# Two mixture-of-experts stages and attention as one program in steps

## The reference

```python
x = x + attn_a(layernorm(x), ...)    # test-time training, two steps with Newton-Schulz; unchanged here
x = x + ffn(layernorm(x), We, be, Wg, bg)
x = x + attn_b(layernorm(x), g, b, w_qkv, w_out, b_out)
x = x + ffn(layernorm(x), We, be, Wg, bg)

def ffn(x, We, be, Wg, bg):          # 8 experts, the best 2 of each token
    gates = softmax(x_flat @ Wg + bg)
    topk_gates, topk_idx = top_k(gates, 2); topk_gates /= sum(topk_gates)
    expert_out = einsum('nd,edo->neo', x_flat, We) + be
    return sum(take_along_axis(expert_out, topk_idx) * topk_gates)

def attn_b(x, g, b, w_qkv, w_out, b_out):   # x (4, 512, 128), 16 heads of 64
    q, k, v = split(((x - mean) / sqrt(var + eps) * g + b) @ w_qkv)
    attn = softmax(where(frame(q) >= frame(k), q k^T / 8, -inf))   # frames of 32 tokens
    return concat_heads(attn @ v) @ w_out + b_out
```

## Time and profile before

| | us |
|---|---|
| median of 3 runs | 888.53 |
| lowest, highest | 884.89, 889.42 |
| the profiled execution, own time | 889.06 |
| its span, first to last instruction | 887.3 |
| mean granted TensorE clock | 0.934 |

### The profile page before, as it was taken

The page is one execution under the profiler, slowest core; times in us unless marked ns, Lnnn a source line. Parts: engine busy times, 40 slices in busy tenths (PEclk is TensorE's granted clock), DMA queues, the critical chain, the costliest instruction groups (busy, mean ns, idle before and its releaser), DMA issues. The chain is left out here.

```text
span 887.3 us, 16341 instructions
## 1 busy us (share of the span) xinstructions
PE 785.5 (89%) x5510; PEld 615.7 (69%) x5512; DVE 564.9 (64%) x1649; ACT 400.4 (45%) x1118; POOL 351.9 (40%) x538
## 2 busy tenths in 40 slices
PE   4659999888999938887868999999999999999786
PEld 2249999757999836676645766777777777777765
DVE  4946565345656574675696777766676666666458
ACT  4733333333333313322255666565556555565224
POOL 4854544014445371600272443343334333343017
PEclk9979999998999969896788999999999999999779
DMA  3030000000000000000000000000000000000001
GB/s 101 1 131 1 0 0 0 1 1 1 1 0 0 1 0 1 1 1 1 1 1 1 1 1 2 1 2 2 1 2 1 2 1 1 3 1 2 1 1 48
DMA packets 9456, 7.02 MB, mean 8 GB/s; under 512 B 1584, under 2 KB 9008, under 8 KB 9264
## 3 DMA queue, kind: packets, MB, share of 16 engines
q1 hardware_dynamic: 9392, 6.19, 2.2%
HBM read 5.14 MB, written 1.05 MB: 7 GB/s over the span
## 5 line engine op out<-in xcount | busy, mean ns | idle before, releaser
L1324 POOL TENSOR_SCALAR t_p_<-t_p_,t_rinv_ 128x128 f32<-128x128 f32 (+3 forms) x256 | 132.8, 535 | 213.2 <-DVE t_rinv_ L1519 213.2
L1512 DVE CUSTOM_DVE_ANT_0 t_p_<-t_S_,t_mask_ 128x128 f32<-128x128 f32 (+3 forms) x256 | 112.9, 488 | 72.7 <-PE t_S_ L1411 69.2
L1354 ACT ACTIVATE t_p_<-t_p_,t_nmin_ 128x128 f32<-128x128 f32 (+3 forms) x256 | 140.0, 551 | 8.7 <-DVE t_nmin_ L1512 8.7
L1359 ACT ACTIVATE t_pT_<-t_T_ 128x384 f32<-128x384 f32 (+1 forms) x96 | 50.7, 528 | 128.5 <-PE t_T_ L1423 128.5
L1423 PEld LDWEIGHTS t_T_<-ident,t_p_ 128*128 128x128 f32 x640 | 68.3, 141 | 44.6 <-POOL t_p_ L1324 28.7
L1411 PE MATMUL t_S_<-t_k_,t_q_ 64*128 64x256 f32 (+3 forms) x512 | 95.0, 469 | 0.0
L1438 PE MATMUL t_O_<-t_pT_,t_v_ 128*64 128x128 f32 x1280 | 91.0, 280 | 0.1
L1423 PE MATMUL t_T_<-ident,t_p_ 128*128 128x128 f32 x640 | 90.9, 281 | 0.0
L1438 PEld LDWEIGHTS t_O_<-t_pT_,t_v_ 128*64 128x64 f32 x1280 | 68.0, 136 | 29.9 <-ACT t_pT_ L1359 26.5
L433 POOL TENSOR_TENSOR g_sp<-g_s,g_t 128x512 f32<-128x512 f32 x32 | 40.9, 1277 | 103.6 <-DVE g_t L554 103.6
L1523 DVE COPY t_pT_<-t_T_ 128x384 f32<-128x384 f32 (+1 forms) x96 | 57.3, 597 | 3.1 <-PE t_T_ L1423 3.0
(11 more groups left out here) (263 smaller groups left out, 1841.2 us busy)
## 6 DMA issues: line engine op xcount, KB each, us to landing
wqkv<-in_L_attn_b_w_qkv_dram SPq DMA_DIRECT2D x1, 1536.0 KB
x<-in_L_attn_a_x_dram SPq DMA_DIRECT2D x4, 256.0 KB, 3.8
out_dram<-x SPq DMA_DIRECT2D x4, 256.0 KB, 2.3
we<-in_L_ffn_We_dram SPq DMA_DIRECT2D x1, 512.0 KB
wout<-in_L_attn_b_w_out_dram SPq DMA_DIRECT2D x1, 512.0 KB
proj<-n_L_attn_a_ttt_proj_dram SPq DMA_DIRECT2D x1, 256.0 KB, 4.9
gv<-n_L_attn_a_ttt_gate_dram SPq DMA_DIRECT2D x1, 256.0 KB, 4.7
gv<-in_L_attn_a_ttt_val_dram SPq DMA_DIRECT2D x1, 256.0 KB, 5.0
```

What stands on the lines that cost most here:

```text
L1324: last = pool.tensor_scalar(pr[:, G.par, h, cols], pr[:, G.par, h, cols], rinv[:, G.par, n:n + 1], 1.0, ALU.mult, ALU.mult)
L1354: act.activation(pr[:, G.par, h, cols], pr[:, G.par, h, cols], ACT.Exp, bias=nmin[:, G.par, n:n + 1], scale=-1.0, accum_out=rsum[:, G.par, ...
L1359: act.activation(pT[:, G.par, 0, G.blocks], psT[:, 0, 0:G.width], ACT.Copy).then_inc(t["eA"], 1)
L1512: dve.tensor_tensor_reduce(pr[:, G.par, h, cols], psS[:, (2 * G.n + h) % 3, at_:at_ + keys], mask[:, SEQ - keys:SEQ], 1.0, -NEG, ALU.add, ...
```

## The change

`moe_phase` and `attention_phase` go; `second_half_phase` does the work of all three stages in one block, in steps from -36 to 129. Attention's group s has step s, 0 to 95, as before. A `Job` is one batch of one expert stage: jobs 0 to 3 are the first stage, 4 to 7 the second. `FRONT` and `EXPERTS` say at which step a job's front (moments, norm, turning, logits, five parts of routing, weights, biases: 12 steps) and its four expert tiles (two steps each) begin. So job 0 comes ahead of attention, job 1's front too, job 7 behind it, and the other work of jobs 1 to 6 stands between pieces of attention. Input moments and norm of each batch, and the outputs of attention, are placed by step too (`in_batch`, `old_output`: four outputs in four steps in a row).

With that, other things change. The weighing of v is done once per pair, for its three groups in a row, and uses a bank of the shared ring, which has three banks now. ScalarE takes four experts of a tile and VectorE four (were three and five). GpSimd forms 1 / sqrt with a power, in place of ScalarE's root and VectorE's reciprocal. Expert biases are per batch: 32 rows and 512 columns, 4 transfers in place of 16. Routing is done per batch on 4 tiles, not on 16 at once.

```diff
+        self.mhalf = sb("mhalf", [P, NT])
...
-        self.beh, self.bel = sb("beh", [P, NT * P], F32R), sb("bel", [P, NT * P], F32R)
+        self.beh, self.bel = sb("beh", [TPB * NE, SEQ], F32R), sb("bel", [TPB * NE, SEQ], F32R)
...
-        self.be = sb("be", [P, NT, P])
+        self.be = sb("be", [TPB * NE, TPB, P])
...
-    LATE_LOADS = 10 + NT
+    LATE_LOADS = 10 + TPB
...
-        c(pool.tensor_tensor(wide(self.beh[:, :]), self.be[:, :, :], times(self.ones, NT), ALU.mult))
+        c(pool.tensor_tensor(wide(self.beh[:, :]), self.be[:, :, :],
+                             self.ones[0:TPB * NE, :].unsqueeze(1).broadcast_to([TPB * NE, TPB, P]), ALU.mult))
         c(pool.tensor_tensor(self.bel[:, :], be, self.beh[:, :].bitcast(F32), ALU.subtract))
...
-    def moe_phase(self, nth):
...
+        FRONT = (-36, -35, 4, 18, 34, 58, 82, 106)
+        EXPERTS = (-24, 0, 16, 30, 46, 70, 94, 118)
+
+        def __init__(self, j):
+            self.j, self.last = j, j >= BATCH
+            self.b, self.par = j % BATCH, j % 2
+            self.rows = slice(self.b * TPB, self.b * TPB + TPB)
+            self.front, self.experts = Kernel.Job.FRONT[j], Kernel.Job.EXPERTS[j]
+
+        def tile(self, s):
+
+            d = s - self.experts
+            return d // 2 if d % 2 == 0 and 0 <= d < 2 * TPB else None
...
-            psS, psT, psO, psP = ps("S", [P, 3, 512]), ps("T", [P, 2, 512]), ps("O", [P, 512]), ps("P", [P, 2, 512])
+            psS, psT, psP = ps("S", [P, 3, 512]), ps("T", [P, 2, 512]), ps("P", [P, 3, 512])
...
+            STEPS = range(Job.FRONT[0], Job.EXPERTS[-1] + 2 * TPB + 4)
+            IN_BATCH = NP * self.NG
+            NORM, TURN, LOGIT, TOP, ROUTE, WEIGHTS, BIAS = 1, 2, 3, 4, 5, 10, 11
...
+            def old_output(s):
+                b, n = s // IN_BATCH - 1, s % IN_BATCH - 5
+                return (b, n) if 0 <= n < TPB and 0 <= b < BATCH else None
+
+            def in_batch(s, step):
+                b = s // IN_BATCH + 1
+                return b if s % IN_BATCH == step and 0 <= b < BATCH else None
...
+                uses += [("eh", J.j * TPB + n) for J, n in tiles(s)]
+                uses += [("el", J.j * TPB + n) for J, n in tiles(s, 1)]
+                uses += [("pv", at(s, LV).pair)] if at(s, LV) and at(s, LV).g == 2 else []
...
-                return psP[:, place[kind, n] % 2, :]
+                return psP[:, place[kind, n] % 3, :]
...
+                def power(kind, n, b):
+                    pool.wait_ge(t["var"], norm_of[kind, n] + 1)
+                    rows = slice(b * TPB, b * TPB + TPB)
+                    pool.tensor_tensor(self.rstd[:, rows], self.lnw[:, 3, rows], self.mhalf[:, rows], ALU.pow).then_inc(t["root"], 1)
+
+                def add_experts(J, n):
+                    i = J.j * TPB + n
+                    pool.wait_ge(m["y"], i + 1)
+                    pool.tensor_tensor(half[:, :, :], y[:, i % 2, 0:2, :], y[:, i % 2, 2:4, :], ALU.add).then_inc(m["z0"], 1)
+                    pool.wait_ge(m["z0"], i + 1)
+                    if i > 1:
+                        pool.wait_ge(m["s"], 4 * (i - 2) + 2)
+                    pool.tensor_tensor(z[:, i % 2, :], half[:, 0, :], half[:, 1, :], ALU.add).then_inc(m["z"], 1)
+
+                def close(J, n):
+                    i = J.j * TPB + n
+                    pool.wait_ge(m["s"], 4 * i + 4)
+                    pool.tensor_tensor(x[:, J.b * TPB + n, :], a[:, i % 2, :], b_[:, i % 2, :], ALU.add).then_inc(m["x"], 1)
...
+                def high(J):
+                    act.wait_ge(m["T"], J.j + 1)
+                    if J.j > 1:
+                        act.wait_ge(m["E"], TPB * (J.j - 1))
+                    act.activation(mh[:, J.par, :], bank("mt", J.j), ACT.Copy).then_inc(m["h"], 1)
...
+                def weigh(J, n):
+                    i = J.j * TPB + n
+                    act.wait_ge(m["c"], J.j + 1)
+                    act.wait_ge(m["H"], i + 1)
+                    if i > 1:
+                        act.wait_ge(m["z0"], i - 1)
+                    for e in range(4):
+                        last = act.activation(y[:, i % 2, e, :], bank("eh", i)[:, tile_of(e)], ACT.Copy,
+                                              scale=wt[:, J.par, n, 4 + e:5 + e])
+                    last.then_inc(m["y"], 1)
...
-                def weigh(G):
-                    pe.wait_ge(t["eA"], G.n + 1)
-                    pe.wait_ge(t["eB"], G.n + 1)
...
+                def weigh(pair):
+                    b, p = divmod(pair, NP)
+                    wait_bank(pe, "pv", pair)
+                    pe.wait_ge(t["ve"], b * 8 + (p // TPB) * TPB + TPB)
+                    for g in range(self.NG):
+                        G = Group(pair * self.NG + g)
+                        pe.wait_ge(t["eA"], G.n + 1)
+                        pe.wait_ge(t["eB"], G.n + 1)
+                        for qt in G.tiles:
+                            for n in range(qt + 1):
+                                for h in range(2):
+                                    d = slice(h * DH, h * DH + DH)
+                                    at_ = (self.FIRST_BLOCK[qt] + n) * P
+                                    last = pe.matmul(bank("pv", pair)[d, tile_of(qt)], v[:, b % 2, n, p * P + h * DH:p * P + h * DH + DH],
+                                                     pT[:, G.par, h, at_:at_ + P], start=(n == 0), stop=(n == qt))
+                    last.then_inc(t["PV"], 1)
...
+                def experts(J, n, kind, first, done):
+                    i = J.j * TPB + n
+                    cols = slice(first, first + 512)
+                    wait_bank(pe, kind, i)
+                    mm3(pe, bank(kind, i), mh[:, J.par, tile_of(n)], ml[:, J.par, tile_of(n)], weh[:, cols], wel[:, cols]).then_inc(done, 1)
+
+                for s in STEPS:
+                    if next_q(s) is not None:
+                        project(next_q(s), "q", 0, t["pq"])
+                    if next_k(s) is not None:
+                        project(next_k(s), "k", HEADS * DH, t["pk"])
+                    if values(s):
+                        project_v(*values(s))
+                    if old_output(s):
+                        output(*old_output(s))
+                    if in_batch(s, 12) is not None:
+                        turn_x(in_batch(s, 12))
+                    for J in jobs(s, TURN):
+                        turn_tokens(J)
+                    for J in jobs(s, LOGIT):
+                        logits(J)
+                    for J in jobs(s, WEIGHTS):
+                        turn_weights(J)
+                    for J in jobs(s, BIAS):
+                        biases(J)
+                    for J, n in tiles(s):
+                        experts(J, n, "eh", 512, m["H"])
+                    for J, n in tiles(s, 1):
+                        experts(J, n, "el", 0, m["E"])
+                    if O and O.g == 2:
+                        weigh(O.pair)
...
+                def accumulate(J, n):
+                    i = J.j * TPB + n
+                    weight = lambda e: wt[:, J.par, n, e:e + 1]
+                    dve.wait_ge(m["c"], J.j + 1)
+                    dve.wait_ge(m["xb"], J.j + 1)
+                    dve.wait_ge(m["E"], i + 1)
+                    if i > 1:
+                        dve.wait_ge(m["x"], i - 1)
+                    for e in range(4):
+                        acc = (a, b_)[e % 2][:, i % 2, :]
+                        if e == 1:
+                            dve.wait_ge(m["z"], i + 1)
+                        if e > 1:
+                            dve.wait_ge(m["s"], 4 * i + e - 1)
+                        so_far = (x[:, J.b * TPB + n, :], z[:, i % 2, :])[e] if e < 2 else acc
+                        dve.scalar_tensor_tensor(acc, bank("el", i)[:, tile_of(e)], weight(e), so_far,
+                                                 ALU.mult, ALU.add).then_inc(m["s"], 1)
...
+                    for J, n in tiles(s, 3):
+                        if not J.last:
+                            stats_of_tokens(J, n)
+                    if old_output(s - 1):
+                        stats_of_output(*old_output(s - 1))
+                    if in_batch(s, 10) is not None:
+                        moments(in_batch(s, 10))
+                    for J in jobs(s, 0):
+                        moments(J.b)
+                    if in_batch(s, 11) is not None:
+                        norm_x(in_batch(s, 11))
+                    for J in jobs(s, NORM):
+                        norm(J)
+                    if next_k(s) is not None:
+                        take_k(next_k(s))
+                    if values(s):
+                        take_v(*values(s))
+                    if old_output(s):
+                        add_output(*old_output(s))
+                    if in_batch(s, 12) is not None:
+                        low_x(in_batch(s, 12))
+                    for J in jobs(s, TURN):
+                        low(J)
+                    for J in jobs(s, LOGIT):
```

(16 more changed lines are left out.)

587 lines of the change are left out of this document (247 added, 340 removed).

## The result

The changed kernel takes 902.49 us (median of 4 runs, 900.42 to 903.73), the kernel before beside it 886.71 (4 runs, 884.66 to 889.42): a ratio of 1.016, 95% interval 1.0134 to 1.0186. It is slower by 15.8 us, where I had forecast 878.2 in all, and it lies above my range.

What follows compares the result with a forecast made beforehand. It took TensorE as full in attention and the expert stages as short of work to overlap. 887.3 - 6.6 - 22 + 47.1 - 8.3 + 8 - 29.1 = 876.4 us span, plus 1.8 outside, 878.2; range 867 to 892.

Steps and rivals of the forecast that it cites:

- A: Expert biases: narrower GpSimd splits let the VectorE instructions at L806 finish sooner; -6.6 us, bounds 0 and 9.1.
- B: Head before attention: first scores wait for batch 0's experts alone, so start about 454 instead of 476.01; -22 us.
- C: Beside attention: experts of jobs 1 to 6 and fronts of jobs 2 to 6 add their TensorE time; +47.1 us.
- D: Attention: weighing v once per pair saves two TensorE gaps at changes of array shape per pair; -8.3 us.
- E: Beside attention: new waits as VectorE gets tight, about 80% busy; +8 us, from 1 to 20.
- F: Tail behind the last weighing: only job 7 is left, 39.0 us instead of 68.2; -29.1 us.
- Rival 1: VectorE sets the pace beside attention, scores waiting for row minima; 897.5 us, or 906 with split waits; chance 0.18.
- Rival 2: TensorE's gaps belong to waits, not shapes: weighing saves 0, each of 68 new pieces brings 0.17; 898 us, chance 0.05.

Runs made afterwards that it cites:

- placed: `slack` with job 1's experts and job 2's front put back beside attention and job 3 shifted; 877.2 us, ratio 0.9871 to the kernel before.
- before_pair: The kernel before with only the weighing of v done in one piece per pair instead of three; 879.0 us, ratio 0.9883.
- slack: The changed kernel, low halves one step later, work of jobs 1, 2 moved into the head, moments and normalizations beside attention in each pair's weighing step; 878.5 us.
- slack_off: `slack` with the moments and normalizations beside attention one step later, in a head pair's second step, and fronts and experts shifted along; 894.5 us, ratio 1.0062.

## Why the prediction was wrong

**A, biases, -6.6: right, 5 to 6 measured.** VectorE's three instructions take 2.65 us at 319.65 instead of 9.09, inside the "under 3.5" that I had set, and the phase behind ends 5.0 us earlier; alone it gives 5.6 to 5.8. The query end is at 397.5 in the mean of the eleven kernels with smaller biases, and at 403.2 and 404.5 in the two with the wide ones.

**B, head, scores near 447: 452.5, 5 us late.** 1.6 of it is A. Another part is GpSimd's power, twice on the way: it took 1.02 us, where I had chosen 0.4 between 0.2 and 1.3, so 1.2 us of the 5. TensorE waits 8.1 us for attention's first normalized tokens (433.55 to 441.64), where I had 2.8 for the norm and 3 for the last sums; 0.6 of that excess is the power again. The rest was not followed.

**C, work that enters attention, +47.1: right, within 1.5 us.** In `placed` TensorE is busy 377.5 us beside attention, 44.1 more than the 333.4 of `before_pair`. 126 of the 144 expert matmuls lie in that stretch, for which the forecast's prices give 47.1 - 4.1 = 43.0. In `slack` it is 371.7 - 333.4 = 38.3, and the prices give 36.8 (111 matmuls, and a front less). Nor was a pair with experts off: in the changed kernel three copies of weighed values stand 11.91 us apart, the forecast had 11.9:

```profile
651.34 0.69 DVE L1491 COPY t_oT_<-t_P_ 128x512 f32<-128x512 f32 x1 [1.64 <-PE t_P_ L1350]
663.25 0.69 DVE L1491 COPY t_oT_<-t_P_ 128x512 f32<-128x512 f32 x1 [2.62 <-PE t_P_ L1350]
675.16 0.69 DVE L1491 COPY t_oT_<-t_P_ 128x512 f32<-128x512 f32 x1 [1.05 <-PE t_P_ L1350]
```

**D, weighing, -8.3: right, -9.3.**

**E, new waits, +8 from 1 to 20: this is the step that failed.** By C and D as measured, 343.1 + 47.1 - 9.3 = 380.9 us are work; the stretch took 407.8, so E was 26.9: 19.5 idle (407.8 less 388.3 busy), and 7.4 more of busy time, which goes with the low clock (with none, `slack` and `placed` have the work of the sum within 1.5 us). Two things were left out. First, I walked through steps with experts and steps with routing, and put moments and normalizations into VectorE's total alone, 11 instructions a front, and attention's own moments. They are the largest pieces: 2 us of moments (7 at 0.21, so 1.5, in the forecast), 1.1 to 1.9 us of normalization, in steps that have no room. An average of 80% said nothing on that; `slack` and `slack_off` have 81% and 79% and lie 13 us apart. Second, I priced stalls at their length, and in three places they cost the clock as well. My range for E reached 20: the idle time alone is just inside, with the clock it is not.

**F, tail, -29.1: nearly right, -26.6**, 41.6 us for 39.0; one power of 1.02 us is in it, and TensorE waits 4.10 us for the first normalized tokens, where I had 2.9 for moments and norm.

**The rivals.** Rival 1 gave 897.5 to 906, and 902.5 lies within; its sign, scores waiting for row minima, came too (6.8 us at the groups of 512 columns, 2.7 at those of 256). Its mechanism, that VectorE's amount sets the pace, is wrong all the same: the amount is nearly the same in `placed` (310 us for 315), 25 us faster. The place of the work set the pace. That 902.5 lies in that rival's range is luck. The remaining error is in how the rivals were built: I weighed the amount against the amount and had no case for bad placement. Rival 2 gave each new piece 0.17 us, 11.6 in all, on top of a D of 0: D was -9.3, and C leaves at most 1.5 for such an addition.

## What to carry to other kernels

When one engine is full, ask of every piece that another engine gets in which step of the full engine's loop it stands, and how long that engine's own work covers it there; a load averaged over the loop does not answer this, and one step further on cost 13 us beside attention here, 16 in all. Work moved beside a full engine is paid at its full length, so count what the emptied stages give back before the move: 43 us against 47 here. Measure the small parts of a large change alone: the two least conspicuous ones held the whole gain, 16 us.
